# A decoder of thirteen stages on one core: choosing experts by halves of the tokens, beside the attention ahead and between blocks

## The chip, the cores and the metric

The kernel is one program on one core of a Trainium2 chip. The metric is device time in microseconds (us) from launch to end. TensorE (PE) multiplies, PEld is its weight load, DVE (VectorE), ACT (ScalarE) and POOL (GpSimd) work on rows, SP (SyncE) issues most transfers. POOL issues the indirect ones, with one address for each row.

## The reference

x has 16 sequences of 256 tokens of 128 numbers, so 4096 tokens, or 32 tiles of 128 tokens. Four layers follow each other, each of a self-attention, a cross-attention and a feed-forward part, with a residual and a layer norm after each part. Two of the feed-forward parts choose experts for each token:

```
# layer 1: 8 experts, 2 for each token; rows are first normalised
xh = (x - mean) / sqrt(var + 1e-6) * gamma[e] + beta[e]
out[e] = relu(xh @ W1[e] + b1[e]) @ W2[e] + b2[e] + x
y = sum over the 2 chosen e of softmax(top 2 of x @ Wg)[e] * out[e]
# layer 3: 16 experts, 4 for each token
logits = -|x - key|^2 + x @ rw.T + rb
y = sum over the 4 chosen e of softmax(top 4 of logits)[e] * (gelu(x @ w1[e] + b1[e]) @ w2[e] + b2[e])
```

## The kernel before, in words

`program` lists thirteen groups of stages. On every engine they run in that order, each stage waiting for `done` of the one before; each stage has one method for each engine, and an engine's instructions are executed in the order in which they are written. `s4` (CrossAttention) stands ahead of the two-of-eight experts `g5`, `s5`; `s11` (WideCross) ahead of the four-of-sixteen experts `g12`, `s12`. Both attentions are written as slots: slot g holds the scores of one piece, the softmax of an earlier one and the output product of a still earlier one. `s4` runs to slot 77, two slots for a batch; `s11` runs slots 6 to 36, one for a tile of 128 tokens. A `Tail` ends each attention: for a chunk c of four tiles the output product, the residual and moments on DVE (`dve_residual`), the inverse root on POOL by `newton` (`pool_root`), the norm on DVE (`dve_norm`), and the transposition into XT (`pe_turn`, `act_turn`). In `s4` chunk c has these in the slots 43 + 4c and after it; in `s11` the residual of chunk c is in slot 4c + 6.

`Gates` (L2212) does the choice for all 32 tiles at once: logits on TensorE as rows (L2262), transposed back (L2266), then on DVE softmax and `dve_choose`, which takes the largest logit, marks its first place and removes it, two or four times. `Dispatch.dve` (L2583 to L2632) makes slots of it: counts by TensorE, running sums over tiles, a first block for each expert (blocks of 128 rows, sorted by expert), and by `pick` the index of each chosen row. Two halves of 16 tiles are sorted separately but are computed together. `XHat` normalises the rows for the eight experts. After `Dispatch.dve` the b2 terms are put on X (L2296, L2303, L2484).

`ChosenExperts` then works in DRAM: `pool` (L3012) scatters rows of XT to L_sorted_rows, one indirect transfer for each tile and choice: 32 or 64 for each half. The first half's go out at once, the second half's one for each block (it waits for `xc`). Each half has NB = 39 or 79 blocks. SP loads a block (L3005); TensorE transposes it (L3049), multiplies it by W1 (L3057) and by W2 (L3066); DVE copies the block's expert out of the table of all experts (L3130) and the transposed rows (L3134, L3137); ACT applies the function (L3082) and copies the result (L3090), which SP stores. At last POOL gathers the results of each token (L3034) and DVE adds them (L3106), for the first half between blocks of the second.

## Time and profile before

| | us |
|---|---|
| median of 3 timed runs | 4725.97 (4720.38 to 4726.91) |
| the profiled execution | 4700.51 |
| its span | 4698.7 |
| TensorE busy | 3596.7 (77%) |
| DVE busy | 2838.3 (60%) |
| ACT busy | 2090.2 (44%) |
| POOL busy | 1134.3 (24%) |

The span runs from the first to the last instruction of one execution, on which the hardware profiler noted every instruction. Busy times can overlap between engines. What ended an idle time is inferred from semaphore events.

### The profile page before, as it was taken

How to read it: one execution, taken by the hardware profiler on the slowest of the kernel's cores; microseconds unless marked ns; L12 is line 12 of the kernel's file. 1: busy time of each engine (PE TensorE's matmuls, PEld its weight loads, DVE VectorE, ACT ScalarE, POOL GpSimd, SP SyncE). 2: the span in 40 equal slices, each digit the busy share in tenths (PEclk: the TensorE clock that was granted, in tenths of full speed). 3: DMA queues.
4: the chain of work that ended last, by engine and by line, in shares of the span. 5: the costliest groups of instructions: out<-in, count | busy, mean ns of one | idle time of the engine just before them, and what ended most of it. 6: DMA issues, size and time to landing. Idle time of an engine off the chain costs nothing. (4 is left out here: it accounts for less than half of the span.)

```text
span 4698.7 us, 87572 instructions
## 1 busy us (share of the span) xinstructions
PE 3596.7 (77%) x31326; PEld 2273.4 (48%) x31326; DVE 2838.3 (60%) x7553; ACT 2090.2 (44%) x4560; POOL 1134.3 (24%) x2203
## 2 busy tenths in 40 slices
PE   5877988877886758369898997579948979837980
PEld 2433553645553448224444453335526766617980
DVE  4974764547784645346776774477745568843453
ACT  2664655223434435136666664435611134414650
POOL 2322221021112254400111101243200041135346
PEclk9987998878986769669999997679968989958995
DMA  5323230112213142211112200423200030032232
GB/s 96 50 37 54 55 53 22 38 25 40 37 16 51 28 131 83 46 24 33 29 32 36 36 20 17 63 41 50 38 10 8 5 108 1 1 101 86 86 87 58
DMA packets 289737, 215.05 MB, mean 46 GB/s; under 512 B 43811, under 2 KB 274560, under 8 KB 289132
## 3 DMA queue, kind: packets, MB, share of 16 engines
q1 hardware_dynamic: 277020, 184.28, 20.4%
q0 software_dynamic: 12288, 25.19, 1.8%
q8 instruction: 253, 4.15, 0.4%
q14 instruction: 176, 1.44, 0.1%
HBM read 61.88 MB, written 45.69 MB: 23 GB/s over the span
## 5 line engine op out<-in xcount | busy, mean ns | idle before, releaser
L1316 ACT ACTIVATE PT<-ps 128x512 f32<-128x512 f32 (+1 forms) x1600 | 811.9, 559 | 513.1 <-PE ps L1376 270.9
L1266 DVE TENSOR_REDUCE M<-ps 128x2 f32<-128x512 f32 x1024 | 655.5, 684 | 288.5 <-PE ps L1250 260.8
L1229 PE MATMUL ps<-SKB 49*128 49x256 bf16 (+2 forms) x3584 | 433.9, 280 | 180.1 <-DMA SKB<-HH 81.2
L1263 DVE TENSOR_REDUCE M<-ps 128x3 f32<-128x384 f32 x768 | 390.6, 550 | 189.3 <-PE ps L1247 123.8
L1411 PE MATMUL ps<-PT,VA 128*9 128x256 f32 (+1 forms) x7168 | 449.9, 370 | 1.5 <-ACT PT L1316 1.0
L1356 PE MATMUL ps<-SKB 51*128 51x256 bf16 (+2 forms) x3584 | 366.2, 271 | 83.7 <-DMA SKB<-MT 65.5
L1229 PEld LDWEIGHTS ps<-SKB 48*128 48x128 bf16 (+1 forms) x3584 | 138.7, 95 | 484.2 <-issue 153.7
L3082 ACT ACTIVATE SKB<-ps,SKB 128x128 f32<-128x128 f32 x944 | 270.2, 371 | 201.6 <-PE ps L3057 186.6
L425 POOL TENSOR_TENSOR NW<-NW 128x4 f32<-128x4 f32 x336 | 70.8, 211 | 1014.9 <-DVE NW L418 987.8
L3130 DVE COPY SKB<-SKB 128x1028 f32 (+1 forms) x236 | 170.2, 721 | 225.6 <-PE ps L3066 127.5
L578 POOL TENSOR_TENSOR FF<-FF,HH 128x512 f32<-128x512 f32 (+1 forms) x118 | 128.8, 1092 | 605.2 <-ACT HH L567 605.0
L3066 PE MATMUL ps<-SKB 128*128 128x128 f32 x1888 | 256.0, 279 | 18.6 <-ACT SKB L3082 13.2
L3057 PE MATMUL ps<-SKB 128*128 128x128 f32 x1888 | 257.8, 281 | 0.0
L3023 POOL DMA_INDIRECT L_sorted_rows<-XT,RR x192 | 203.9, 1062 | 206.9 <-DVE RR L2623 81.6
L1411 PEld LDWEIGHTS ps<-PT,VA 128*9 128x9 f32 x7168 | 155.1, 91 | 199.8 <-issue 96.0
L3034 POOL DMA_INDIRECT SKB<-L_sorted_results,RR x192 | 192.4, 1002 | 235.4 <-DMA L_sorted_results<-SKB 101.7
L1356 PEld LDWEIGHTS ps<-SKB 50*128 50x128 bf16 (+1 forms) x3584 | 177.2, 98 | 143.3 <-DMA SKB<-MT 75.1
L3066 PEld LDWEIGHTS ps<-SKB 128*128 128x128 f32 x1888 | 234.1, 195 | 22.6 <-ACT SKB L3082 15.7
L3057 PEld LDWEIGHTS ps<-SKB 128*128 128x128 f32 x1888 | 235.7, 196 | 0.1
L2843 PEld LDWEIGHTS ps<-SKB 128*128 128x128 f32 x1536 | 187.8, 193 | 46.1 <-issue 45.9
L655 PE MATMUL ps<-idf,TV 128*128 128x128 f32 x1088 | 175.5, 285 | 34.4 <-ACT TV L646 17.4
L1307 ACT ACTIVATE PT<-ps 128x768 f32<-128x768 f32 x128 | 103.8, 811 | 210.0 <-DVE ps L1386 210.0
(369 smaller groups left out, 6995.6 us busy)
## 6 DMA issues: line engine op xcount, KB each, us to landing
SKB<-HH SPq DMA_DIRECT2D x1224, 64.0 KB
SKB<-HH SPq DMA_DIRECT2D x576, 32.0 KB
PT<-L_sorted_rows SPq DMA_DIRECT2D x236, 64.0 KB
L_sorted_results<-SKB SPq DMA_DIRECT2D x236, 64.0 KB
L_sorted_rows<-TV SPq DMA_DIRECT2D x2, 5056.0 KB, 30.9
SKB<-in_L3f_w SPq DMA_DIRECT2D x32, 256.0 KB
L_sorted_rows<-TV SPq DMA_DIRECT2D x2, 2496.0 KB, 15.5
SKB<-scratch SPq DMA_DIRECT2D x2, 2048.0 KB, 10.9
```

What stands on the lines that cost most here:

```text
L1229: k = e.matmul(self.mx_bank(m + i)[:, o:o + n], K.QS[self.set(c)][64 * i:64 * i + rows, s, 256 * bb + 128 * qt:256 * bb + 128 * qt + 128], ...
L1263: k = e.tensor_reduce(K.M3[n % 2][:, hh, 0:3], mx[:, 0:384].rearrange("p (a k) -> p a k", a=3), axis=AX.X, op=ALU.max)
L1266: k = e.tensor_reduce(K.M3[n % 2][:, hh, 0:2], mx.rearrange("p (a k) -> p a k", a=2), axis=AX.X, op=ALU.max)
L1316: e.activation(K.PT[:, x % 4, n * i:n * i + n], self.st_bank(x, i)[:, 0:n], ACT.Exp, bias=0.0, scale=self.scale).then_inc(*self.exp.inc())
L1356: k = e.matmul(self.st_bank(x, i)[:, 256 * kt:512 - lo if kt else 256], k1, q1, start=kt == 0, stop=plain and kt == 1)
L1411: k = e.matmul(K.PS[32 * i:32 * i + 9, 6, 256 * g + lo:256 * g + 256], K.VA[self.set(c)][:, (2 * bb + kt) * 16 + 8 * (i % 2) + 2 * j + i / ...
L2843: k = e.matmul(K.PS[:, 4 + m % 2, 128 * i:128 * i + 128], self.HB[m % 3][:, hc, 128 * i:128 * i + 128], self.WE[m // 8 % 3][:, 512 + 128 * ...
L3023: e.indirect_dma_start(self.XS[h], bass.IndirectOffsetOnAxis(ap=D.IDX[:, q:q + 1], axis=0), K.XT[:, 128 * t:128 * t + 128], None).then_inc ...
L3034: e.indirect_dma_start(self.YG[i % 8], None, self.YS[c // 4], bass.IndirectOffsetOnAxis(ap=D.IDX[:, q:q + 1], axis=0)).then_inc(*self.gath ...
L3057: k = e.matmul(K.PS[:, 2 + m % 2, 128 * hc:128 * hc + 128], self.WT[m % 3][:, 128 * hc:128 * hc + 128], self.XC[m % 3], start=True, stop=True)
L3066: k = e.matmul(K.PS[:, 4 + m % 2, 0:128], self.HB[m % 3][:, hc, :], self.WT[m % 3][:, 512 + 128 * hc:640 + 128 * hc], start=hc == 0, stop= ...
L3082: k = e.activation(self.HB[n % 3][:, hc, :], K.PS[:, 2 + n % 2, 128 * hc:128 * hc + 128], self.func, bias=self.WT[n % 3][:, 1024 + hc:1025 ...
```

## The change

The choice, the slots and the scatter are done for each half of the tokens by itself. `ChosenGates` takes the place of `Gates`, `Dispatch` and `XHat` for these two stages. Its work for each engine is a generator that is stepped. The steps of the first half stand in the last slots of the attention ahead (`at` is the first slot, `rate` the steps in a slot, `each` the scatters in a slot); those of the second half stand between blocks (`own` steps in a block). The logits come as 16 products with the tokens as weights, without transposition. The b2 terms, for the eight experts together with the scaling of X, stand between blocks 20 and 46. The second half's scatters no longer wait for blocks. The weights of the experts are loaded in slots of the attentions, and the zeros between sorted rows of the two-of-eight stage are written in the third group. Softmax, dispatch tables and gathered rows have other places in SBUF (`Room`). `WideCross.pool` is written by slots, so that scatters stand between the roots of the tail.

```diff
     def dve(self, e):
         self.join(e)
         for g in range(self.lead, self.slots):
+            if self.beside:
+                self.beside.dve_beside(e, g)
             self.dve_slot(e, g)
...
             self.pool_slot(e, g)
+            if self.beside:
+                self.beside.pool_beside(e, g)
...
+        if self.beside is not None:
+            if self.P + 16 <= g < self.P + 21:
+                self.beside.sp_expert(e, g - self.P - 16)
+            if g == self.P + 36:
+                e.wait_ge(*self.scored(6))
+                self.beside.sp_expert(e, 5)
+                self.beside.sp_expert(e, 6)
+            if g == self.P + 41:
+                e.wait_ge(*self.scored(7))
+                self.beside.sp_expert(e, 7)
...
+def choose(e, dv, G, v, best, removed, tiles, made=None):
+    E = G.E
+    sh = [128, tiles, E]
+    rev = G.rev[:, 0:E].rearrange("p (o e) -> p o e", o=1).to_broadcast(sh)
+    for k in range(G.top):
+        if k > 0:
+            e.tensor_reduce(G.ZE, v, axis=AX.X, op=ALU.max).then_inc(*dv.inc())
+            e.wait_ge(*dv.now())
+            best = G.ZE
+        e.tensor_tensor(G.EQ, v, spread(best, sh, "p (t o) -> p t o"), ALU.is_equal).then_inc(*dv.inc())
+        e.wait_ge(*dv.now())
+        e.tensor_tensor(G.FIRST, G.EQ, rev, ALU.mult).then_inc(*dv.inc())
+        e.wait_ge(*dv.now())
+        yield
+        e.tensor_reduce(G.Z, G.FIRST, axis=AX.X, op=ALU.max).then_inc(*dv.inc())
+        e.wait_ge(*dv.now())
+        e.tensor_tensor(G.OH[k], G.FIRST, spread(G.Z, sh, "p (t o) -> p t o"), ALU.is_equal).then_inc(*dv.inc())
+        e.wait_ge(*dv.now())
+        if k < G.top - 1:
+            left = G.LEFT[k % 2]
+            e.scalar_tensor_tensor(out=left, in0=G.OH[k], scalar=removed, in1=v, op0=ALU.mult, op1=ALU.add
+                                   ).then_inc(*dv.inc())
+            v = left
+        if k > 0:
+            o = e.tensor_tensor(G.MK, G.OH[0] if k == 1 else G.MK, G.OH[k], ALU.add)
+            if made and k == G.top - 1:
+                o.then_inc(*made.inc())
+            else:
+                o.then_inc(*dv.inc())
+        e.wait_ge(*dv.now())
+        yield
...
+        self.masked = 2 + 2 * top
+    def counts_at(self, gap):
+        return self.masked + max(gap, 7 if self.normed else 2)
+    def idx_at(self, gap, k):
+        return self.counts_at(gap) + 5 + k
...
+    def pe(self, e, h, gap):
+        K, W, E = self.K, self.W, self.E
+        n = 16 * E
+        e.wait_ge(*W.at)
+        if self.router:
+            e.wait_ge(*self.router.made.at(0))
+        gw = self.router.gw if self.router else W["gw"]
+        pj = K.pj_take(e)
+        if self.router and h == 0:
+            e.matmul(pj[:, n:n + E], W["one"], self.router.sq, start=True, stop=True)
+        for i in range(16):
+            t = 16 * h + i
+            if i % 4 == 0:
+                e.wait_ge(*self.ahead.tail.xt.at(t // 4))
+            k = e.matmul(pj[:, E * i:E * i + E], K.XT[:, 128 * t:128 * t + 128], gw, start=True, stop=True)
+        k.then_inc(*self.lmm.inc())
+        K.pj = self.lg.at(h)
+        for _ in range(self.counts_at(gap)):
+            yield
+        e.wait_ge(*self.mask.at(h))
+        pj = K.pj_take(e)
+        mk = self.MK.rearrange("p t e -> p (t e)")
+        e.matmul(pj[:, 0:n], W["triu"], mk, start=True, stop=True)
+        e.matmul(pj[:, 256:256 + n], W["one"], mk, start=True, stop=True).then_inc(*self.counted.inc())
+        K.pj = self.read.at(h)
...
+    def act(self, e, h, gap):
+        K = self.K
+        yield
+        e.wait_ge(*self.sub.at(h))
+        e.activation(self.EX, self.EX, ACT.Exp, bias=0.0, scale=1.0).then_inc(*self.exp.inc())
+        if self.normed:
+            for _ in range(self.counts_at(gap)):
+                yield
+            e.wait_ge(*self.root.at(h))
+        e.wait_ge(*self.lmm.at(h))
+        for c in range(4 * h, 4 * h + 4):
+            if self.normed:
+                for t in range(4 * c, 4 * c + 4):
+                    i = t - 16 * h
+                    k = e.activation(K.XT[:, 128 * t:128 * t + 128], K.X[:, t, :], ACT.Identity,
+                                     bias=self.SHIFT[:, i:i + 1], scale=self.RSD[:, i:i + 1])
+            else:
+                k = e.activation(K.xt(c).rearrange("p (a b) -> p a b", a=4), K.xc(c), ACT.Copy, bias=0.0, scale=1.0)
+            if c % 4 == 3:
+                k.then_inc(*self.rows.inc())
+            yield
...
+    def dve(self, e, h, gap):
+        K, W, E, dv = self.K, self.W, self.E, self.K.dv
+        sh = [128, 16, E]
+        e.wait_ge(*self.lmm.at(h))
+        logits = K.PS[:, 7, 0:16 * E].rearrange("p (t e) -> p t e", t=16)
+        if self.router:
+            if h == 0:
+                e.tensor_tensor(W["rbb"], W["rbb"], K.PS[:, 7, 16 * E:17 * E], ALU.add).then_inc(*dv.inc())
+                e.wait_ge(*dv.now())
+            e.tensor_tensor(self.LG, logits, W["rbb"].rearrange("p (o e) -> p o e", o=1).to_broadcast(sh), ALU.add
+                            ).then_inc(*self.lg.inc())
+        else:
+            e.tensor_copy(self.LG, logits).then_inc(*self.lg.inc())
+        e.wait_ge(*self.lg.at(h))
+        yield
+        e.tensor_reduce(self.S1, self.LG, axis=AX.X, op=ALU.max).then_inc(*dv.inc())
+        e.wait_ge(*dv.now())
+        e.tensor_tensor(self.EX, self.LG, spread(self.S1, sh, "p (t o) -> p t o"), ALU.subtract).then_inc(*self.sub.inc())
+        yield
+        for _ in choose(e, dv, self, self.LG, self.S1, NEG, 16, self.mask):
+            yield
+        e.wait_ge(*self.mask.at(h))
+        e.wait_ge(*self.exp.at(h))
+        e.tensor_tensor(self.EX, self.EX, self.MK, ALU.mult).then_inc(*dv.inc())
+        e.wait_ge(*dv.now())
+        e.tensor_reduce(self.S1, self.EX, axis=AX.X, op=ALU.add).then_inc(*dv.inc())
+        e.wait_ge(*dv.now())
+        yield
+        e.reciprocal(self.S2, self.S1).then_inc(*dv.inc())
+        e.wait_ge(*dv.now())
+        e.tensor_tensor(self.gates(h), self.EX, spread(self.S2, sh, "p (t o) -> p t o"), ALU.mult).then_inc(*self.g.inc())
...
+            e.wait_ge(*self.ahead.tail.x.at(4 * h + 3))
+            for part in range(4):
+                for i in range(8 * (part % 2), 8 * (part % 2) + 8):
+                    if part < 2:
+                        k = e.bn_stats(self.ST[:, i, :], K.X[:, 16 * h + i, :])
+                    else:
+                        k = e.bn_aggr(self.MV[:, i, :], self.ST[:, i, :])
+                k.then_inc(*dv.inc())
+                e.wait_ge(*dv.now())
+                yield
+            if h == 1:
+                e.wait_ge(*self.root.at(0))
+            root_seed(e, K, self.NW[:, 0, :], self.NW[:, 1, :], self.MV[:, :, 1], 1e-6).then_inc(*self.seed.inc())
...
+            pk = self.PK[:, 16 * k:16 * k + 16]
+            self.pick(e, k, by_expert(pos), pk)
+            e.tensor_copy(self.IDX[:, col], pk).then_inc(*self.idx.inc())
+            yield
...
+    def pe_beside(self, e, g):
+        if g >= self.at:
+            self.step("pe", self.D.pe(e, 0, 2 * self.rate), self.rate)
+    def act_beside(self, e, g):
+        if g > self.at:
+            self.step("act", self.D.act(e, 0, 2 * self.rate), self.rate)
+    def dve_beside(self, e, g):
+        if g == self.at - 1:
+            self.D.dve_first(e)
+        if g > self.at:
+            self.step("dve", self.D.dve(e, 0, 2 * self.rate), self.rate)
+    def pool_beside(self, e, g):
+        if g > self.at:
+            self.step("pool", self.pool_first(e), 1)
+    def pool_first(self, e):
+        D, top, gap = self.D, self.top, 2 * self.rate
+        seeded, n = (D.counts_at(gap) - 1) // self.rate, 0
+        while n < D.idx_at(gap, 0) // self.rate:
+            if n == seeded and D.normed:
+                D.pool_root(e, 0)
+            yield
+            n += 1
+        for i in range(16 * top):
+            if i > 0 and i % self.each == 0:
+                yield
+            self.pool_scatter(e, 0, i)
+    def pool_scatter(self, e, h, i):
+        K, D = self.K, self.D
+        k, t = i // 16, 16 * h + i % 16
+        if i == 0:
+            e.wait_ge(*self.zeroed.at(0))
+            e.wait_ge(*D.rows.at(h))
+        if i % 16 == 0:
+            e.wait_ge(*D.idx.at(self.top * h + k))
+        q = 32 * k + t
+        e.indirect_dma_start(self.XS[h], bass.IndirectOffsetOnAxis(ap=D.IDX[:, q:q + 1], axis=0),
+                             K.XT[:, 128 * t:128 * t + 128], None).then_inc(self.scattered[h].sem, 16)
...
+        self.rest("pool")
+        if D.normed:
+            D.pool_root(e, 1)
+        for i in range(16 * top):
+            self.pool_scatter(e, 1, i)
...
+            if n >= 1:
+                for _ in range(self.own):
+                    next(second, None)
+            c = self.b2_at.get(n)
+            if c is not None:
+                self.pe_gates_turn(e, c)
+            c = self.b2_at.get(n - 3)
+            if c is not None:
+                self.pe_b2(e, c)
...
+    def dve_b2(self, e, c):
+        K, D = self.K, self.D
+        pj = K.PS[:, 7, :].rearrange("p (a b) -> p a b", a=4)
+        e.wait_ge(*self.b2.at(c))
+        e.wait_ge(*D.rows.at(c // 4))
+        if self.normed:
+            for i in range(4):
+                t = 4 * c + i
+                k = e.scalar_tensor_tensor(out=K.X[:, t, :], in0=K.X[:, t, :], scalar=D.SG[:, t:t + 1], in1=pj[:, i, :],
+                                           op0=ALU.mult, op1=ALU.add)
+        else:
+            k = e.tensor_tensor(K.xc(c), K.xc(c), pj, ALU.add)
+        k.then_inc(*self.x.inc())
...
+            if n == NB:
+                for _ in second:
+                    pass
+            if n % NB == 0:
+                e.wait_ge(*self.D.blocks.at(n // NB))
...
+            if 2 <= n < NB:
+                for _ in range(self.own):
+                    next(second, None)
+            c = self.b2_at.get(n - 5)
+            if c is not None:
+                self.dve_b2(e, c)
...
+        o = self.o
+        e.wait_ge(*self.abc.at(3))
+        e.wait_ge(*self.tail.biased.at(7))
+        for x in (0, 1, 2):
+            self.beside.sp_expert(e, x)
+        e.wait_ge(*o.at(23))
+        for x in (12, 13):
+            self.beside.sp_expert(e, x)
+        e.wait_ge(*self.u.at(31))
+        e.wait_ge(*self.st.at(27))
+        for x in (3, 4, 14, 15):
+            self.beside.sp_expert(e, x)
+        e.wait_ge(*o.at(27))
+        self.beside.sp_expert(e, 8)
+        e.wait_ge(*self.st.at(31))
+        for x in (5, 6, 7):
+            self.beside.sp_expert(e, x)
+        e.wait_ge(*o.at(31))
+        for x in (9, 10, 11):
+            self.beside.sp_expert(e, x)
...
-        for c in range(8):
-            self.tail.pool_root(e, c)
+        for g in range(6, 37):
+            if g % 4 == 2:
+                self.tail.pool_root(e, g // 4 - 1)
+            if self.beside:
+                self.beside.pool_beside(e, g)
...
-        g5 = Gates(K, s4, W[5], 8, "L1", top=2)
-        s5 = ChosenExperts(K, g5, W[5], g5.dispatch, ("L1f_w1", "L1f_w2", "L1f_b1"), ACT.Relu)
+        g5 = ChosenGates(K, s4, W[5], 8, "L1", 2, Room([K.SKB[:, 10240:14336]]), None)
+        s5 = ChosenExperts(K, s4, W[5], g5, ("L1f_w1", "L1f_w2", "L1f_b1"), ACT.Relu, at=59, rate=3, each=3, own=2)
...
-        g12 = Gates(K, s11, W[12], 16, "L3", top=4)
-        s12 = ChosenExperts(K, g12, W[12], g12.dispatch, ("L3f_w1", "L3f_w2", "L3f_b1"), ACT.Gelu, last=True)
-        groups = ((s0,), (s1,), (g2, s2), (s3,), (s4,), (g5, s5), (s6,), (s7,), (s8,), (g9, c9, s9), (s10,), (s11,),
-                  (g12, s12))[:stop]
+        room = Room([K.GG[:, :]] + [t[:, :] for t in K.OT] + [v[:, :, :].rearrange("p a b -> p (a b)") for v in K.VA]
+                    + [K.BIG[:, 8192:10520]])
+        g12 = ChosenGates(K, s11, W[12], 16, "L3", 4, room, K.HH[0][:, :, :].rearrange("p a b -> p (a b)"))
+        s12 = ChosenExperts(K, s11, W[12], g12, ("L3f_w1", "L3f_w2", "L3f_b1"), ACT.Gelu, at=21, rate=4, each=5, own=1,
+                            last=True)
...
+        s4.beside = s5 if stop > 5 else None
+        s11.beside = s12 if stop > 12 else None
...
-                if n == 5:
-                    s4.done(e)
+                if n == 2 and stop > 5:
+                    s1.done(e)
                     s5.pool_zero(e)
...
-                if n == 12:
-                    W[n].load(e)
-                if n == 5:
-                    s5.sp_zero(e)
+                if n == 11 and stop > 12:
+                    W[12].load(e)
...
+                if n == 2 and stop > 5:
+                    s5.sp_zero(e)
```

## Rows read from the trace of the kernel before

**Rows 1.** The page, part 1: busy us, share of the span, instructions.
```profile
PE 3596.7 (77%) x31326; PEld 2273.4 (48%) x31326; DVE 2838.3 (60%) x7553; ACT 2090.2 (44%) x4560; POOL 1134.3 (24%) x2203
```

**Rows 2.** Busy time by stretch: us, each engine, PE clock, DMA share, GB/s.
```profile
1598.70:1640.50 41.80, 22.69 (x170) 13.13 (x169) 20.84 (x92) 13.80 (x29) 9.55 (x48) 0.76 0.01 1
1640.50:1676.70 36.20, 21.63 (x84) 9.93 (x84) 23.82 (x117) 19.18 (x44) 3.88 (x15) 0.64 0.90 275
1676.70:1727.30 50.60, 16.30 (x66) 12.06 (x65) 18.96 (x54) 2.94 (x5) 37.19 (x32) 0.50 0.14 47
1727.30:1811.00 83.70, 83.30 (x720) 82.78 (x721) 48.09 (x87) 55.06 (x209) 39.27 (x34) 0.97 0.31 94
...
4112.00:4168.40 56.40, 21.54 (x86) 8.78 (x86) 31.99 (x68) 12.19 (x17) 0.00 (x0) 0.62 0.49 158
4168.40:4255.00 86.60, 15.94 (x65) 12.20 (x65) 21.14 (x30) 2.35 (x4) 64.09 (x64) 0.50 0.15 50
4255.00:4424.00 169.00, 163.59 (x1422) 162.58 (x1422) 80.33 (x168) 110.26 (x415) 69.19 (x68) 0.97 0.31 93
```

**Rows 3.** Order of time, start and us: scatters and blocks begin.
```profile
1676.70 1.22 POOL L3023 DMA_INDIRECT L_sorted_rows<-XT,RR  x1 [22.09 <-DVE RR L2623]
...
1727.32 0.66 PE L3049 MATMUL ps<-idf,PT 128*128 128x128 f32 x2 [20.42 <-issue]
...
4168.44 1.07 POOL L3023 DMA_INDIRECT L_sorted_rows<-XT,RR  x1 [59.54 <-DVE RR L2623]
...
4250.76 0.96 POOL L3023 DMA_INDIRECT L_sorted_rows<-XT,RR  x1 [0.31 <-issue]
...
4254.99 1.36 PE L3049 MATMUL ps<-idf,PT 128*128 128x128 f32 x3 [51.92 <-DMA PT<-L_sorted_rows]
```

**Rows 4.** Order of time: DVE in the last slots of both attentions.
```profile
1616.31 1.11 DVE L337 TENSOR_SCALAR X<-RR,MV,RSD 128x128 f32<-128x128 f32 x4 [2.48 <-POOL RSD L431]
...
4074.68 1.22 DVE L3530 TENSOR_REDUCE M<-PT 128x16 f32<-128x1024 f32 x1 [1.12 <-ACT PT L3523]
...
4088.94 0.17 DVE L418 TENSOR_SCALAR NW<-NW 128x4 int32<-128x4 int32 x1
...
4105.36 0.17 DVE L418 TENSOR_SCALAR NW<-NW 128x4 int32<-128x4 int32 x1
...
4108.93 1.12 DVE L337 TENSOR_SCALAR X<-RR,MV,RSD 128x128 f32<-128x128 f32 x4 [3.40 <-POOL RSD L431]
```

**Rows 5.** Order of time: operations of the choice on DVE.
```profile
1640.51 6.29 DVE L2743 BATCH_NORM_STATS2 SKB<-X 128x6 f32<-128x128 f32 x32 [1.95 <-issue]
...
1654.83 0.42 DVE L2374 TENSOR_TENSOR PT<-PT,SKB 128x256 f32<-128x256 f32 x1
...
1671.44 0.28 DVE L2590 TENSOR_TENSOR SKB<-SKB 128x128 f32<-128x128 f32 x1
...
4180.90 1.46 DVE L2628 TENSOR_TENSOR SKB<-RR,WB 1x1264 f32<-1x1264 f32 x1
```

**Rows 6.** Order of time: the expert copy on DVE among blocks.
```profile
1728.54 0.70 DVE L3130 COPY SKB<-SKB 128x1030 f32 x1 [0.32 <-issue]
...
1756.69 0.70 DVE L3130 COPY SKB<-SKB 128x1030 f32 x1 [0.68 <-issue]
...
4330.59 0.85 DVE L3130 COPY SKB<-SKB 128x1028 f32 x1 [0.89 <-issue]
...
4332.48 0.88 DVE L3130 COPY SKB<-SKB 128x1028 f32 x1 [0.85 <-issue]
```

**Rows 7.** A scatter and a table load (start, us); waits (total, times, longest).
```profile
1683.40 7.04 POOL L3023 DMA_INDIRECT L_sorted_rows<-XT,RR  x1 [0.30 <-issue]
...
4262.00 1.28 ACT L3082 ACT_TABLE_LOAD   x1 [61.06 <-remote]
...
DVE X L2484 <- remote: 48.3, 5, 14.7
DVE SKB L3130 <- remote: 31.5, 12, 3.5
```

491 lines of the change are left out of this document (246 added, 245 removed).

## The prediction

> **What bounds the kernel now.** I read the page first, then the table of stretches around the two stages with chosen experts, then the order of time in them, then the waits. The page [rows 1] says only that TensorE is busiest and no engine is full: shares over thirteen stages decide nothing. The stretches do [rows 2]. Between the attention and the two-of-eight experts nothing overlaps: 36.2 us in which DVE chooses (23.8 busy), then 50.6 us in which POOL scatters (37.2 busy) and TensorE waits. Before the four-of-sixteen experts the same two parts take 56.4 and 86.6 us. The attentions end at 1640.5 and 4112.0; POOL's first scatters start at 1676.70 and 4168.44, TensorE's first blocks at 1727.32 and 4254.99 [rows 3], which ends the two stretches. So two heads of 86.8 and 143.0 us, 229.8 in all, are what can be hidden. The blocks behind are TensorE's: 83.3 of 83.7 us busy, and 163.6 of 169.0 [rows 2], a block each 1.89 us (4332.48 - 4330.59) [rows 6]. Whatever is put between blocks costs once the little slack there is used. The gathers that end the kernel are not touched.
>
> **The change part by part.** *One half's choice on DVE.* Half of the tokens makes operations of 256 elements with sixteen experts and of 128 with eight: 0.42 and 0.28 us, 0.04 between them [rows 5]. Sixteen experts, four chosen: 25 operations of the choice, 5 of the weights, 10 of copying, running sums and positions, 16 of the picks, 56 x 0.46 = 26; some 22 small ones at 0.2 make 4; the block table 2 x 1.46 = 3: 33 us, 23 of them before the first index. Eight experts, two chosen: 34 x 0.32 = 11, small ones 3.5, table 1, and 16 of the 32 statistics, 16/32 of 6.29 and about 1 = 4: 19.5 us. The whole choice is thus not less DVE work than before, only cut in two.
>
> *First half in the wide attention (slots 22 to 30 of 36).* DVE is the bound there: 1.12 us of idle in about every second slot of 6.3 us [rows 4]. Of the 23 us before the first index some 3 vanish in it. The step stands at the head of slot 27, which began at 4074.68 - 12.6 = 4062: first scatter at 4082 instead of 4168. A scatter takes (4250.76 - 4168.44)/63 = 1.31 us [rows 3]; beside DVE's long operations I take 1.5. POOL, in its written order, issues 15 (4104), then waits for the seed of chunk 6, which DVE's inserted work moves from 4088.94 by 28 to 4117; the root is 3.4 us (4105.53 to 4108.93) [rows 4]; 20 scatters to 4147; the root of chunk 7, whose seed (4105.36, then 4133) has been waiting, to 4151; the last 29 to 4189. From last scatter to first block it was 4.2 us [rows 3]: 4193. The attention itself ends at 4155, covered by the scatters. Gain 62 us.
>
> *First half in the attention ahead (slots 60 to 67).* DVE is busy 20.8 of the last 41.8 us [rows 2], so much of the 19.5 fits, but not in slots 60 to 62, and DVE's order puts steps ahead of the norm: 3 us for the first slots, 4 for the norm of chunk 5, 2 for ACT waiting for the root of the row norms. The norm of chunk 5 stood at 1616.31 [rows 4], slot 66 a microsecond later: first scatter at 1627. Six scatters 1635, root of chunk 6 1638.5, twelve 1654, root of chunk 7 1657.5, fourteen 1676, first block 1680. Gain 47 us.
>
> *Second half between blocks.* DVE waits 0.85 us in a block of the last stage and 0.68 in the other, of which 0.32 stays even when nothing holds it [rows 6]: slack 0.53 and 0.36 us. Last stage: 33 blocks with a step each, 33 - 33 x 0.53 = 15 us. Other: 12 blocks with two, 19.5 - 12 x 0.36 = 15. TensorE gets 16 products for the logits, two counts and, for b2, 8 x 12 records; a block is 17 records in 1.89, so 0.11 each: 10.7 for b2, 5 for the rest, per stage. In the last stage half of it lies beside DVE-bound blocks (8 with DVE's b2 sum); in the other, where b2 falls into TensorE-bound blocks, 13. Exp between Gelus on ACT: two table loads of 1.28 us [rows 7]: 3. Together 26 and 28, 54 us. Bounds: with perfect packing 36; with no overlap at all 33 + 19.5 + 31 + 3 + 14 for DVE's b2 sums (8 of 512 elements, 0.7 us by the same line, and 32 of 128) = 100.
>
> *Trains of scatters beside critical work.* The second scatters are no longer one per block but back to back, 32 and 64, 126 us at 1.31. No row shows such a train beside blocks. From below it costs nothing: 38 scatters, one per block, left TensorE 97% busy [rows 2]. From above, rows 7: with trains running, DVE's b2 sum waited 48.3 us in five waits that no engine ended, of 137 us of scattering (50.6 + 86.6), and one scatter took 7.04 us beside unbroken DVE work. Nearest are the gathers in bursts of eight among blocks: the expert copy waited 31.5 us in twelve such waits. I take 15 us, both ends kept.
>
> The Trainium skill, "SBUF — State Buffer", section on the two physically separate sides with its box on DVE blocking SWDGE, says that DVE and GpSimd share one port pair by exclusive lock, and that a two-port copy keeps GpSimd from writing descriptors. The 7.04 us scatter [rows 7] agrees; the one at 4168.44, which ran beside DVE's picks in 1.07 us [rows 3], does not show it. By that rule each expert copy and train exclude each other, which is the second rival below.
>
> *Moved and free.* Expert weights (24 x 0.53 MB), issued by SP, go into attention slots whose DMA share is 0.01, so they leave the heads; SP's waits for freed parts of the tile stand behind the last stacks, so nothing is late. If they queued ahead of a shift's transfer, 0.53 MB at the 158 GB/s of the head, 3 us, and the scores need it two slots later. Zero stores go to the third stage, behind its strips and beside its last experts. Gates, the logits' transposes and 32 row scalings in the heads vanish: they lay under the scatter and pay nothing. The second half is scattered before block 39 or 79 is due (it ends about block 34 and 62). TensorE's granted clock was 0.76 where it was busy 22.7 of 41.8 us and 0.97 in the blocks [rows 2]. Blocks that wait for DVE leave it 1.9 of some 3.0 us, so part of them will be at 1.2 GHz; their records then take about DVE's pace, which I leave unpriced and cover by the range.
>
> **The sum.** 62 + 47 = 109 gained, 54 + 15 = 69 paid: 40 us. The profiled execution took 4700.51 (span 4698.7), so 4660.5; the median of the timed runs is 4725.97, 25 us above it, and I keep that distance: 4686 us. Own range: paid 50 to 85, gain 24 to 59, 4667 to 4702.
>
> **The rivals.** *Packing is better.* Paid 36 and nothing for the trains: gain 73, 4653. For it: steps are cut small, and two blocks of buffering even them out. Against: TensorE is 97% busy already.
>
> *The trains wait with DVE (slower).* If during the 126 us of second scatters DVE gets through only each 10 to 15 us, as the sum's longest wait of 14.7 says, blocks stand for the train's whole length: gain 109 - 54 - 126 = -71, 4797. It decides slower once the trains stop the blocks for more than 55 of 126 us. For it: rows 7. Against: DVE picked on beside the first scatters of the head [rows 3], and the expert copies among gathers waited 3.5 us at the most. In its milder form, waits of 48.3/137 of the train's length, it takes 44 us instead of 15: gain 11, 4715.
>
> *The head is not hidden.* If POOL in slots 27 to 36 gets hardly a scatter in because DVE's 1.22 us operations follow one another, 50 scatters start at 4125 only: 4125 + 64 x 1.31 + 7 + 4 = 4220, 27 us later; with 5 us in the other stage the gain is 8, 4718.
>
> **How the numbers follow.** Forecast 0.55, better packing 0.17, mild trains 0.12, head not hidden 0.06, trains that stop the blocks 0.10. A measurement tells 0.2%, 9.5 us, from no change. Faster (under 4716.5): 0.55 + 0.17 + 0.07 + 0.02 = 0.81; same 0.09; slower 0.10. Eight in ten: 4640 (better packing and 13 us more) to 4728, leaving out the stopped blocks and a tail below.
>
> **What would show it.** First scatters about 1627 and 4082 (the latter 14 earlier by what the first stage gains, 47 - 28 - 5); no stretch of over 10 us without TensorE between attention and blocks but some 22 us in the first and 38 in the last stage; first blocks at 1680, and 4193 - 14 = 4179. Expert copies 2.4 us apart in the last stage's first 35 blocks and 3.0 in the other's first 13, later 1.9. Unexplained waits of DVE under 25 us in the trains. Wrong would be: scatters of several microseconds in the attention, blocks stretched to 5 us and more, or an attention that ends after its scatters do.

## The result, and the profile after

The changed kernel is slower: 4803.81 us (4797.35 to 4805.70, 4 runs) against 4726.44 us (4720.38 to 4728.93, 4 runs), ratio 1.0163 [1.0146, 1.0181], where 4686 was forecast. The profiled execution took 4803.26 us around a span of 4801.4, so it stands at its median; that of before stood 25 us under its own. Between the two spans lie 102.7 us, between the medians 77.4, so up to 25 us of what the traces show below come from that quick execution of before. Later runs on chips 5, 8, 11 and 15 (the number of the first run's chip is not known) split this result: on chip 8 it came again, 1.0164, and on chip 15 the same kernel is *faster*, 0.9961 and 0.9952.

The page of the kernel after, part 1, answers to [rows 1]: TensorE's busy time rose by 29 us, its share fell.

```profile
PE 3625.6 (76%) x31366; PEld 2314.0 (48%) x31366; DVE 2841.9 (59%) x7683; ACT 2080.0 (43%) x4552; POOL 1118.5 (23%) x2217
```

The view of busy time by stretch, kernel after (columns as in [rows 2]). Lines one to four are the two-of-eight stage: the tail of the attention, the wait for scatters, blocks beside the second half's choice, the second half's scatters. The last four are the same of the four-of-sixteen stage.

```profile
1640.50:1677.40 36.90, 11.22 (x54) 6.97 (x52) 10.81 (x46) 9.00 (x22) 23.37 (x43) 0.55 0.14 47
1677.40:1697.40 20.00, 1.26 (x5) 0.90 (x5) 0.95 (x3) 0.60 (x1) 12.74 (x13) 0.50 0.29 86
1697.40:1744.10 46.70, 36.70 (x238) 35.16 (x238) 29.49 (x112) 21.24 (x75) 3.77 (x14) 0.80 0.13 37
1744.10:1789.80 45.70, 16.28 (x100) 14.75 (x99) 7.03 (x16) 7.24 (x28) 31.81 (x32) 0.64 0.18 60
...
4155.40:4198.40 43.00, 16.91 (x108) 14.68 (x106) 20.25 (x46) 7.14 (x8) 26.45 (x45) 0.70 0.38 117
4198.40:4238.60 40.20, 2.21 (x9) 1.59 (x9) 1.02 (x3) 0.60 (x1) 27.26 (x29) 0.50 0.16 55
4238.60:4296.40 57.80, 49.38 (x368) 46.97 (x368) 35.08 (x99) 31.11 (x104) 0.00 (x0) 0.91 0.16 45
4296.40:4383.10 86.70, 16.48 (x85) 12.99 (x84) 8.16 (x18) 5.39 (x21) 61.75 (x64) 0.56 0.16 54
```

In the fourth line of each stage POOL issues a train, that is scatters one right after the other, and TensorE, which should do blocks, is busy for 16 us of 46 and of 87. The heads are mostly hidden, as meant: the order of time in the kernel after, first scatter and first block of both stages, against [rows 3].

```profile
1646.96 1.21 POOL L3149 DMA_INDIRECT L_sorted_rows<-XT,SKB  x1 [8.86 <-ACT XT L2880]
...
1697.23 0.91 PE L3218 MATMUL ps<-idf,PT 128*128 128x128 f32 x2 [18.61 <-DMA PT<-L_sorted_rows]
...
4130.73 1.07 POOL L3149 DMA_INDIRECT L_sorted_rows<-XT,SKB  x1 [1.14 <-DVE SKB L3017]
...
4237.48 0.91 PE L3218 MATMUL ps<-idf,PT 128*128 128x128 f32 x2 [37.81 <-DMA PT<-L_sorted_rows]
```

Since everything before a stage moves its absolute times (the two executions are 6.3 us apart at the first mark; on chip 15 it is 1.4), I compare distances. Each is in us from SP's issue of a weight load in the same stage or just ahead of it (the gate weights of the two-of-eight stage; the linear attention's `wkv`), in the profiled execution named. Chip 15 ran both kernels side by side.

| from the mark | before | after | before, chip 15 | after, chip 15 |
|---|---|---|---|---|
| two of eight: attention ends | 123.0 | 155.5 | 119.6 | 155.7 |
| first block | 211.8 | 175.4 | 207.4 | 175.6 |
| block 40 (second half) | 284.7 | 318.5 | 280.8 | 283.2 |
| last block | 384.5 | 422.0 | 369.4 | 376.3 |
| four of sixteen: attention ends | 664.0 | 711.1 | 666.7 | 711.3 |
| first block | 809.0 | 750.2 | 811.5 | 750.5 |
| block 80 (second half) | 964.3 | 1016.8 | 960.4 | 938.4 |
| last block | 1141.6 | 1203.4 | 1121.2 | 1100.9 |

First blocks come 36.4 and 58.8 us earlier, 95.2 gained. Blocks 1 to 40 then take 143.1 instead of 72.9 us and blocks 1 to 80 take 266.6 instead of 155.3; second halves take 3.7 and 9.3 more: 194.5 paid. Net 99.3 of the 102.7 between the spans.

Where it is lost, in the order of time (kernel after, DVE's expert copy, one a block):

```profile
1716.88 0.70 DVE L3366 COPY SKB<-SKB 128x1030 f32 x1 [0.44 <-issue]
1720.00 0.70 DVE L3366 COPY SKB<-SKB 128x1030 f32 x1 [0.76 <-DVE SKB L2936]
...
1768.75 0.70 DVE L3366 COPY SKB<-SKB 128x1030 f32 x1 [12.26 <-issue]
1789.85 0.70 DVE L3366 COPY SKB<-SKB 128x1030 f32 x1 [19.89 <-remote]
...
4301.58 0.73 DVE L3366 COPY SKB<-SKB 128x1028 f32 x1 [0.33 <-issue]
4313.69 0.70 DVE L3366 COPY SKB<-SKB 128x1028 f32 x1 [10.19 <-remote]
4383.10 0.70 DVE L3366 COPY SKB<-SKB 128x1028 f32 x1 [67.14 <-remote]
```

The first pair is choice between blocks: 3.12 us a block instead of 1.9 [rows 6]. The others are stops: two blocks in 81.5 us. "Remote" means that the profile found no releaser. TensorE's and ScalarE's rows in the same stretch lead to it. Here x1 or x8 is the number of matmuls in the row:

```profile
4317.84 0.37 PE L3226 MATMUL ps<-SKB 128*128 128x128 f32 x1 [1.78 <-issue]
4319.24 0.37 PE L3226 MATMUL ps<-SKB 128*128 128x128 f32 x1 [1.03 <-issue]
...
4323.44 0.37 PE L3226 MATMUL ps<-SKB 128*128 128x128 f32 x1 [1.03 <-issue]
4325.54 0.37 PE L3226 MATMUL ps<-SKB 128*128 128x128 f32 x1 [1.73 <-issue]
4363.20 2.08 PE L3235 MATMUL ps<-SKB 128*128 128x128 f32 x8 [37.29 <-issue]
```
```profile
4362.01 1.14 ACT L3306 ACTIVATE SKB<-ps,SKB 128x128 f32<-128x128 f32 x4 [48.14 <-remote]
4383.01 0.28 ACT L3314 ACTIVATE SKB<-ps 128x128 f32<-128x128 f32 x1 [19.86 <-remote]
```

Matmuls of one block that otherwise start 0.11 us apart start 1.40 us apart and more, waiting for nothing the profile shows; scatters start 1.26 us apart. ScalarE can use their result only at 4362.0, 36 us after the last of them (4325.54 + 0.37) by the profile, whose ends of matmuls are modelled. The scatters end at 4377.4. So in this stretch TensorE stops; ScalarE waits for it, and DVE, SP and in the end TensorE wait in a ring. Transfers are not what is late: the packets of SP's store and load issued at 4313.90 and 4314.26 had moved by 4316. The scatters keep their 0.96 us throughout and the long stop has no copy in it: it isn't DVE and GpSimd that shut each other out. The Trainium skill's rule on that ("SBUF — State Buffer", the section on the two physically separate sides), cited in the prediction, is not what these rows show. The scatter of 7.04 us [rows 7], which the prediction laid to that rule, came on chip 15 too, again in 7.04 us beside the same 8.49 us of DVE work, where no train stops anything: it is another effect, and prices no train. Whether DVE, given work, would have been slowed as TensorE was, these rows can't tell; a later experiment does.

### The profile page after: what moved, and what is told of

Its sections match the earlier page's. It is cut to its first block and busy times, and to the rows that moved or that the text cites. A ratio compares the mean times of both kernels' runs of the same rounds, so it can differ in the third digit from the quotient of the medians.

```text
span 4801.4 us, 87829 instructions
## 1 busy us (share of the span) xinstructions
PE 3625.6 (76%) x31366; PEld 2314.0 (48%) x31366; DVE 2841.9 (59%) x7683; ACT 2080.0 (43%) x4552; POOL 1118.5 (23%) x2217
## 5 line engine op out<-in xcount | busy, mean ns | idle before, releaser
L3235 PE MATMUL ps<-SKB 128*128 128x128 f32 x1888 | 267.7, 287 | 82.9 <-issue 44.9
L3235 PEld LDWEIGHTS ps<-SKB 128*128 128x128 f32 x1888 | 244.2, 202 | 88.7 <-issue 46.3
L3201 POOL DMA_INDIRECT PT<-L_sorted_results,SKB x192 | 191.7, 999 | 394.0 <-DMA L_sorted_results<-SKB 249.9
L3226 PE MATMUL ps<-SKB 128*128 128x128 f32 x1888 | 271.3, 289 | 9.3 <-issue 9.3
L3226 PEld LDWEIGHTS ps<-SKB 128*128 128x128 f32 x1888 | 247.5, 204 | 10.1 <-issue 9.9
L3149 POOL DMA_INDIRECT L_sorted_rows<-XT,SKB x192 | 188.3, 981 | 137.6 <-DVE SKB L3017 63.4
L2663 PEld LDWEIGHTS ps<-SKB 128*128 128x128 f32 x1536 | 186.3, 192 | 46.1 <-issue 45.8
## 6 DMA issues: line engine op xcount, KB each, us to landing
L_sorted_rows<-TV SPq DMA_DIRECT2D x2, 2496.0 KB, 20.4
```

Source lines behind the costliest of these rows:

```text
L2663: k = e.matmul(K.PS[:, 4 + m % 2, 128 * i:128 * i + 128], self.HB[m % 3][:, hc, 128 * i:128 * i + 128], self.WE[m // 8 % 3][:, 512 + 128 * ...
L3149: e.indirect_dma_start(self.XS[h], bass.IndirectOffsetOnAxis(ap=D.IDX[:, q:q + 1], axis=0), K.XT[:, 128 * t:128 * t + 128], None).then_inc ...
L3201: e.indirect_dma_start(self.YG[i % 8], None, self.YS[c // 4], bass.IndirectOffsetOnAxis(ap=D.IDX[:, q:q + 1], axis=0)).then_inc(*self.gath ...
L3226: k = e.matmul(K.PS[:, 2 + m % 2, 128 * hc:128 * hc + 128], self.WT[m % 3][:, 128 * hc:128 * hc + 128], self.XC[m % 3], start=True, stop=True)
L3235: k = e.matmul(K.PS[:, 4 + m % 2, 0:128], self.HB[m % 3][:, hc, :], self.WT[m % 3][:, 512 + 128 * hc:640 + 128 * hc], start=hc == 0, stop= ...
```

## The experiments

Theory A: scatters issued back to back stop TensorE. Rivals: B, each scatter costs blocks the same wherever it lies; C, pacing (letting each scatter go only when a given block is done) only moves the wait. A burst is a short train. Ratios are to the kernel before on the same chip, with 95% intervals.

**Pace the second half's scatters** (chip 5).
```
         for i in range(16 * top):
+            e.wait_ge(*self.xc.at(self.ready + i * (self.NB - 2 - self.ready) // (16 * top)))   # ready: 12 and 21
             self.pool_scatter(e, 1, i)
```


> The changed kernel, but the second half's scatters are paced: scatter i waits until block ready + i*(NB-2-ready)/count has been turned and copied (one per 1.9 us block or fewer), in both stages. Theory A (scatters issued back to back stop TensorE, so that DVE and ScalarE wait 'remote'; one alone between blocks costs nothing): the stops of 20 us (two-of-eight) and 67+10 us (four-of-sixteen) in the DVE's waits for the expert copy go, 'remote' there falls from 134.5 us to under 30, and the time falls by 85 to 115 us to 4690 to 4720. Rival B (every scatter costs the blocks about 1.1 us of TensorE or DMA wherever it lies): the same 96 scatters cost the same 100 us in small pieces, the time stays 4780 to 4810. Rival C (pacing only makes the second half start late): the blocks run at 1.9 us but a gap of 20 to 60 us stands before the second half's first block; 4730 to 4770.

0.9970 [0.9958, 0.9981]; no remote wait at the expert copy. In this ratio it lies where A put it, and alone it would have looked like proof of A; in microseconds, 4658, it lies below every forecast.

**Bursts of 8** (chip 5): `i` in the wait above becomes `i - i % 8`.

> As the paced kernel, but the same scatters come in bursts of 8 back to back, each burst let go by the block at which its first would have come (4 bursts and 8 bursts). Theory A: each burst of 8 stops TensorE for about 5 to 7 us (the before kernel's bursts of four indirect DMAs show TensorE's signals 1.4 to 2.4 us late), so 12 bursts cost 50 to 90 us against the paced kernel, in pieces of 5 to 8 us. Rival B: the same time as paced and as the changed kernel.

0.9965 [0.9951, 0.9979], again no stop. A had promised 50 to 90 us.

**A pause between unpaced scatters** (chip 5): one memset after each scatter, in the second half alone.
```
             self.pool_scatter(e, 1, i)
+            e.memset(K.TV[:, 0:512], 0.0).then_inc(*K.po.inc())
+            e.wait_ge(*K.po.now())
```


> The changed kernel, unpaced second half, but GpSimd writes a 128x512 tile (one memset, no DMA) between two scatters, so that they come some 1.8 to 2.4 us apart without any tie to the blocks. Theory A (it is back-to-back issue that stops TensorE): the stops of 20 and 77 us go or shrink to a third though the train is unpaced, and the time is 4690 to 4740. If what counts is that GpSimd is never idle, whatever it does, or that the scatters are not tied to the blocks, the stops stay and grow with the train (+60 us): 4820 to 4880.

0.9975 [0.9965, 0.9984].

**Plain DMAs** (chip 5). This version leaves out the sorting of the second half.
```
+        if h == 1:
+            e.dma_start(self.XS[h][128 * i:128 * i + 128, :], K.XT[:, 128 * t:128 * t + 128]
+                        ).then_inc(self.scattered[h].sem, 16)
+            return
...
```


> The changed kernel, but the second half's scatters are plain DMAs from GpSimd's queue: 128 rows to 128 rows in order, not to the chosen slots (so the rows of the second half are not sorted; everything else as before). It tells whether the indirect form matters. Theory A1 (descriptors that GpSimd makes in software for any DMA, back to back): the same stops, 4790 to 4810. Theory A2 (only the indirect form, which reads an index for each row, stops TensorE): no stops, 4690 to 4725.

0.9975 [0.9965, 0.9985]. Four different edits, one result, and the kernel before at 4669 us instead of 4726: chip 5 could not tell the theories apart, and the change itself has not run there. So theory D: the stops belong to the chip.

**The change itself, and the kernel before, for a trace** (chip 15).

> The changed kernel itself, unaltered, as a control beside the others of this call, since the kernel before was 1.2% quicker in the first four experiments' call than beside the first run of the change. If the stops of 20 and 77 us in the trains belong to the kernel (theory A), they are here again and the ratio is 1.014 to 1.020. If they belong to the chip on which it ran (theory D: there one kernel's unpaced train is stopped, here it isn't), 'remote' at the expert copy is under 30 us and the ratio is 0.995 to 1.000, as for the four variants.

> The kernel before, unaltered, for its trace on this call's chip: the ratio is 1.000 by construction. It is to show which stages are shorter where the kernel before takes 4669 us than where it takes 4726: by theory D the head before its first block (in the first trace 86.8 and 143.0 us, with 48.3 us of 'remote' waits of DVE beside the scatters) and the block stages, by a theory of a quicker clock all TensorE-bound stages alike.

0.9961 [0.9947, 0.9976] and 1.0005 [0.9994, 1.0017]. Theory D holds: the same kernel that lost 77 us gains 17. The kernel before is quicker here in the stages with indirect DMAs and hardly elsewhere: its last blocks come 15.1 and 20.4 us earlier from the marks (table). What A missed is that the stops need both the train and the kind of chip. (Chip 15 ran at two times with one result, chips 5, 8 and 11 once each; that it is the chip and not the moment is read from this, not shown.) Busy time by stretch in the change on chip 15, both trains of scatters beside blocks:

```profile
1740.00:1783.80 43.80, 42.04 (x361) 40.10 (x361) 24.80 (x53) 26.52 (x100) 34.07 (x32) 1.00 0.34 103
...
4251.70:4336.80 85.10, 81.63 (x673) 77.82 (x672) 46.38 (x98) 48.26 (x179) 65.59 (x64) 0.96 0.33 102
```

TensorE is busy for 42.0 of 43.8 and 81.6 of 85.1 us beside trains of the same length (34.1 and 65.6 us of POOL) that leave it 16 us elsewhere.

**Gathers paced too** (chip 15; scatters in bursts of 8).
```
+                if c < 4:
+                    e.wait_ge(*self.xc.at(self.NB + 8 + i * (self.NB - 14) // (16 * top)))
                 e.indirect_dma_start(self.YG[i % 8], None, ...
```


> The kernel with the second half's scatters in bursts of 8, and the first half's gathers paced too, one let go per block in place of bursts of four. In the traces each burst of four gathers goes with a block of 3.3 to 5.2 us. If back-to-back issue is what stretches them, the second half's blocks run at 1.9 to 2.1 us each: 10 to 25 us less than the same kernel with gathers in bursts (ratio to before 0.992 to 0.995). If it is the sum's own work on DVE between the blocks, nothing: 0.996 to 0.997.

0.9959 [0.9946, 0.9971]: nothing gained against the change. The second half of the last stage took 161.2 us against 162.5.

**First half's scatters held until the attention has issued its work** (chip 15; scatters of the second half in bursts of 8): in `pool_first`, 64 times `yield` ahead of the scatters.

> The kernel with bursts of 8, but the first half's scatters are kept until the attention ahead has issued all its own work; choice and slots stay between its slots. If scatters in the attention's tail are what lengthens it (its end moved from 1640.5 to 1677 and, less the shift, from 4112 to 4155), the attentions end 15 to 35 us earlier and the 32 and 64 scatters (1.26 us each, 40 and 81 us) follow them: first blocks 5 to 10 and 15 to 30 us later than with scatters inside, ratio 1.001 to 1.006. If it is DVE's choice that lengthens them, the ends stay and the scatters' 20 and 40 us inside the attention are lost: ratio 1.005 to 1.012.

1.0056 [1.0039, 1.0073]. From the marks the attentions end at 145.7 and 697.6. So of their lengthening on chip 15 (36.1 and 44.6 us), the scatters make 10.0 and 13.7, less than the 15 to 35 expected, and what stays with them held, the choice above all, 26.1 and 30.9. First blocks come 13.5 and 30.5 us later: letting scatters into the attention is worth it. This kernel's last norm of the attention, first scatter and first block in the last stage:

```profile
4148.94 1.12 DVE L337 TENSOR_SCALAR X<-RR,MV,RSD 128x128 f32<-128x128 f32 x4 [3.40 <-POOL RSD L431]
...
4149.44 1.07 POOL L3150 DMA_INDIRECT L_sorted_rows<-XT,SKB  x1 [0.54 <-issue]
...
4233.42 0.86 PE L3221 MATMUL ps<-idf,PT 128*128 128x128 f32 x2 [82.12 <-DMA PT<-L_sorted_rows]
```

**The second half's choice in the wait for the first half's scatters** (chip 15).
```
 pe, dve:  second = self.D.pe(e, 1, ...)            # dve the same
+          for _ in second:
+              pass                                  # ahead of the blocks, not one step a block
 act:     +for _ in range(self.D.counts_at(2 * self.own) + 1 if self.normed else 8):
+              next(second, None)
 pool:    +e.wait_ge(*self.xc.at(1 + 7 * i // 8))    # ahead of scatter i of the second half
```


> The changed kernel with the second half's choice and slots moved once more: out of the blocks into the stretch between the attention's end and the first block, where DVE stands idle for the first half's scatters (17.8 us in the two-of-eight stage, 37.5 us in the four-of-sixteen), and the second half's scatters one per block from block 1 on. If choice between blocks is what the blocks pay (39 scatter-free blocks took 34.3 us longer and 79 took 39.1 us longer than in the kernel before on the same chip), 50 to 70 us go and the ratio to before falls from 0.996 to 0.981 to 0.987. If the blocks pay for the scatters beside them instead, at most 15 us go: 0.993 to 0.996. If the second half's choice pushes the first block back by its own length, nothing goes: 0.995 to 1.000.

0.9912 [0.9889, 0.9935]: a smaller gain than the 0.981 to 0.987 hoped for and a larger one than the rival's 0.993, so neither account has the size. It is under the change, which ran beside it (medians 22.5 us apart, and the times of the two don't overlap):

> The changed kernel again, a control. If this call's chip is of the kind on which the kernel before takes some 4725 us, theory A (trains of scatters stop TensorE there) says ratio 1.014 to 1.020 with 'remote' waits of DVE over 100 us at the expert copy; where the kernel before takes some 4670 us, ratio 0.995 to 0.998 and under 30 us, as in the call before. Any other pairing of the two (a slow before with a quick change) breaks the theory that the same property of the chip makes both.

> The change with the second half's scatters one per block, again. On a chip where the trains stop TensorE, theory A says that pacing alone brings the ratio from 1.016 down to 0.995 to 1.002. On the other kind of chip it is worth nothing (0.996 to 0.998), as on the first chip that had it.

0.9952 [0.9933, 0.9971] and 0.9969 [0.9955, 0.9983], the change and the paced change. In the last stage block 80 comes 913.7 us from the mark instead of 937.5 (the change beside it) and blocks among the first 35 are 2.13 us apart instead of 2.75; the two-of-eight stage's block 40 comes at 271.1 instead of 282.6. The wait for scatters had held room for the whole second choice. Its first blocks on TensorE:

```profile
4177.89 1.03 PE L3221 MATMUL ps<-idf,PT 128*128 128x128 f32 x2 [15.95 <-DMA PT<-L_sorted_rows]
4180.90 0.45 PE L3221 MATMUL ps<-idf,PT 128*128 128x128 f32 x1 [1.99 <-DVE SKB L3380]
```

The wait for the first block's rows is 16.0 us where it was 37.9 (4193.10 in the change on chip 15).

**On chip 8, before at 4716 us.** Three kernels side by side: the change as control, the bursts of 8, and the last version (second choice in the wait, scatters one per block) with gathers paced as well.

> The changed kernel, as the control of this call. Before near 4725 us: ratio 1.014 to 1.020, DVE's 'remote' waits at the expert copy above 100 us. Before near 4670 us: ratio 0.994 to 0.998, none.

> The second half's scatters in bursts of 8. Where trains stop TensorE (before near 4725 us), each of the 12 bursts costs 5 to 7 us by theory A (the first few of a train are free, then TensorE stands until its end): ratio 1.002 to 1.010, between paced and unpaced. If what counts is only the total of scatters beside blocks, 1.014 to 1.018. Where the kernel before takes 4670 us: 0.995 to 0.998, as before.

> The kernel with the second half's choice in the wait for the first half's scatters, and besides the first half's gathers paced one by one over the second half's blocks. Where the kernel before takes 4670 us, pacing gathers was worth nothing in sum (0.9959 against 0.9965), so this should be 0.988 to 0.993 as without it. Where the kernel before takes some 4725 us, its bursts of four gathers held TensorE's signals back by 1.4 to 2.4 us each, so that there the pacing gives 10 to 30 us more: 0.978 to 0.990. The rival (paced gathers finish later than bursts and push the end) gives 0.994 to 0.998 on either.

1.0164 [1.0132, 1.0196], 1.0082 [1.0063, 1.0102] and 0.9886 [0.9864, 0.9907]. The first result is reproduced, and here the form of the train sets the price. What DVE waited for ahead of the expert copy (us, times), in the change, in the bursts of 8:

```profile
  PE ps L3235: 159.3, 133
  remote: 146.2, 21
```
```profile
  PE ps L3238: 165.4, 113
  remote: 101.5, 34
```

Blocks 1 to 80 took 259.6, 233.9 and (last version) 177.9 us; on chip 15 the change took 187.9. Over that, a burst costs (233.9 - 187.9)/8 = 5.8 us, as expected, and the one train of 64 costs 71.7. Against the same burst version on chip 5 (186.9) it is 5.9 a burst. The first burst is nearly free, the later ones are not. The sixth in the order of time, scatters and then expert copies:

```profile
4395.03 0.96 POOL L3150 DMA_INDIRECT L_sorted_rows<-XT,SKB  x1 [11.43 <-DVE SKB L3376]
...
4404.33 0.95 POOL L3150 DMA_INDIRECT L_sorted_rows<-XT,SKB  x1 [0.30 <-issue]
4415.60 0.95 POOL L3150 DMA_INDIRECT L_sorted_rows<-XT,SKB  x1 [10.31 <-DVE SKB L3376]
```
```profile
4395.75 0.73 DVE L3369 COPY SKB<-SKB 128x1028 f32 x1 [1.00 <-PE ps L3238]
4398.66 0.70 DVE L3369 COPY SKB<-SKB 128x1028 f32 x1 [1.99 <-PE ps L3238]
4402.34 0.86 DVE L3369 COPY SKB<-SKB 128x1028 f32 x1 [2.78 <-remote]
4406.71 0.70 DVE L3369 COPY SKB<-SKB 128x1028 f32 x1 [3.31 <-remote]
4409.00 0.70 DVE L3369 COPY SKB<-SKB 128x1028 f32 x1 [1.40 <-PE ps L3238]
```

Four blocks take 13.3 us, where the same four on chip 5 take 7.6. Bursts against one train would leave a weaker B alive, one in which each scatter costs something wherever it lies. The last version closes it: the same 64 indirect scatters, one per block on the same chip, cost the blocks 4.1 us (165.8 from the third expert copy to the 80th, 161.7 on chip 15), and DVE's remote waits at the copy in these blocks are 2.1 us in it and 75.9 in the change. C is out as well: no gap stands before the second half's first block, whose expert copy comes 1.9 us after the one before.

The last version also shows that it isn't TensorE alone. Its second choice runs on DVE beside the last unbroken scatters of the first half. Small copies of the running sum, on chip 15 and then on chip 8:

```profile
4166.11 0.15 DVE L2999 COPY VA<-VA 128x1 f32<-128x1 f32 x1
4166.38 0.29 DVE L2999 COPY SKB<-VA 128x2 f32<-128x2 f32 x1
```
```profile
4202.03 0.15 DVE L2999 COPY VA<-VA 128x1 f32<-128x1 f32 x1 [1.18 <-issue]
4203.43 0.17 DVE L2999 COPY SKB<-VA 128x2 f32<-128x2 f32 x1 [1.17 <-DVE VA L3000]
```

They start 0.27 us apart on chip 15 and 1.40 us apart on chip 8; 1.40 us is also the pace at which TensorE's matmuls started above. The chain from L2993 to L3005 takes 1.4 us on chip 15 and 7.7 on chip 8, though its operations last as long, and the third expert copy comes 14.4 us after the first block's transposition instead of 3.6. So theory A is too narrow: beside a train, DVE is slowed too.

**On chip 11, before at 4712 us.** Pause, plain form, and the last version without paced gathers.

> The changed kernel, second half unpaced, one GpSimd memset of 128x512 between two scatters. Where the kernel before takes over 4710 us: if TensorE is stopped by indirect DMAs issued without a pause, the stops of 20 and 80 us go and the ratio is 0.998 to 1.006; if a busy GpSimd is enough, they stay or grow with the train: 1.016 to 1.030. Where the kernel before takes 4670 us: 0.996 to 0.999, as the first time, and nothing is told apart.

> The changed kernel with the second half's scatters as plain DMAs of GpSimd (rows in order, so the second half isn't sorted). Where the kernel before takes over 4710 us: if the descriptors of any GpSimd DMA stop TensorE, 1.010 to 1.018; if it takes the indirect form, 0.998 to 1.004. Where it takes 4670 us: 0.996 to 0.999.

> The second half's choice in the wait for the first half's scatters, its scatters one per block, gathers in bursts of four. Where the kernel before takes over 4710 us: 5 to 20 us more than the version with paced gathers, so 0.990 to 0.994. Where it takes 4670 us: 0.989 to 0.993, as the first time.

0.9954 [0.9937, 0.9971], 0.9957 [0.9939, 0.9975], 0.9927 [0.9907, 0.9947]. The first two gain more than was expected of a chip of chip 8's kind. The change itself did not run on chip 11; that it is of that kind is read from the kernel before's time and from gathers in bursts of four, in the second halves, beside which all of DVE's remote waits lie (ahead of the expert copy, version with the pause; chips 5 and 15 have none):

```profile
  PE ps L3237: 141.4, 106
  remote: 30.8, 12
```

In the version with the pause the same 64 indirect scatters ran untied to blocks on a GpSimd that never rests. The order of time there, POOL and TensorE:

```profile
4258.25 0.96 POOL L3149 DMA_INDIRECT L_sorted_rows<-XT,SKB  x1 [0.28 <-POOL TV L3192]
4259.21 0.54 POOL L3192 MEMSET TV<- 128x512 f32 x1
4260.03 1.10 POOL L3149 DMA_INDIRECT L_sorted_rows<-XT,SKB  x1 [0.28 <-POOL TV L3192]
```
```profile
4265.34 1.06 PE L3237 MATMUL ps<-SKB 128*128 128x128 f32 x8
4266.23 0.27 PE L3220 MATMUL ps<-idf,PT 128*128 128x128 f32 x1
4266.34 1.06 PE L3228 MATMUL ps<-SKB 128*128 128x128 f32 x8
```

Scatters 1.8 us apart (2.0 on average) and matmuls in rows of eight in 1.06 us: blocks 1 to 80 took 189.7 us, and 191.4 in the same version on chip 5. If chip 11 is of chip 8's kind, a pause of 0.8 us is enough, and neither a busy GpSimd nor the tie to the blocks matters. Plain DMAs, 0.6 us apart (64 in 38.3 us), don't stop TensorE either (187.6 us, 187.7 on chip 5), though that train was half as long, so form and length are not parted. And pacing the gathers, worth nothing on chip 15, is worth 16.6 us in the last stage on chip 8: its second half took 165.5 us with it and 182.1 in the change beside it (179.2 without it on chip 11).

## Why the prediction was wrong

- *Heads, right in the last stage.* 62 and 47 us forecast, 58.8 and 36.4 measured (61.0 and 31.8 on chip 15). In the two-of-eight stage the first scatter was due at 1627 and came at 1646.96, 6.3 us of it the execution's shift. ScalarE's sixteen scalings of rows had to follow the root (1637.7) and stood between the attention's own work, so that they ended at 1646.1, where I had 2 us; DVE's and POOL's inserted work made the attention 32.5 us longer where I had 19.5 us of DVE fitting into its gaps. Of the signs of being wrong, "an attention that ends after its scatters do" did not come; "blocks stretched to 5 us and more" did, up to 69 us.
- *Second half between blocks, sized too low.* 28 and 26 us forecast; chip 15, where no train stops anything, gives 38.7 and 40.7 (blocks of both halves). Blocks were 3.2 and 2.75 us apart against 3.0 and 2.4. On chip 15 TensorE's 32 logit records took 6.9 us, 0.22 each, where 0.11 was taken from full blocks: they come behind the wait for scatters, in which TensorE stands, at a granted clock of 0.50 (stretch 1677.40 to 1697.40 above; 0.50 too in chip 15's 1693.6 to 1702.0), the lower of its two levels, 1.2 GHz. The rest I lay to DVE's choice and b2 sums, which fitted less well than the slack promised; no run parts them.
- *Trains of scatters beside blocks: the step that failed.* I took 15 us, "both ends kept". It measured 194.5 - 79.4 = 115.1 us between the first chip's pair of traces and chip 15's (35.2 and 79.9); by the medians, which are free of the quick execution of before, the two pairs differ by 77.4 + 16.6 = 94.0 us, and chip 8's and chip 15's by 88.3. The row that priced it was there: DVE's b2 sum waited 48.3 us in five waits that no engine ended, beside the same trains [rows 7]. In the kernel before on chip 15 the b2 sum has no such wait; TensorE ended all of its waits (us, times, longest):

```profile
DVE X L2484 <- PE ps L2303: 41.9, 20, 4.0
```

So those five were TensorE's results coming late. I spread them over the scattering and then took a lighter row as nearest, of gathers "in bursts of eight"; but only the first eight come together, the others in fours. And [rows 7] came from a stage in which little else ran; in blocks each such stop holds four engines. The "38 scatters, one per block" that left TensorE 97% busy (there are 64 in that stage) were paced, and pace, as the bursts, the pause and the last version show, makes the difference.
- *The rival.* "The trains wait with DVE" forecast 4797 at a chance of 0.10; 4803.8 came. Its place was right and its size near, its mechanism not: DVE does not shut out GpSimd, TensorE stops. That the time came so close is in part luck: its terms were 109, 54 and 126, those of the traces 95, 79 and 115, and the sum of these, -99, is not the -77 of the medians either.
- *The range.* 4640 to 4728 left that rival out because one reading of a price was preferred, though its price of 126 us would alone have turned the sign. On the other kind of chip the forecast's sign is right and its size still over: 0.9961 against 4686/4726 = 0.9915.

The version that beats both kernels is the second choice in the wait, scatters one per block and gathers paced: 0.9886 on the chip where the change is 1.0164. With the gathers paced it ran on chip 8 alone; without, it is 0.9912 on chip 15 and 0.9927 on chip 11.

## What to carry to other kernels

Taking a pacing wait out of a queue of indirect DMAs is an edit of its own: price the train beside the work that it will run beside, from the "remote" waits of the trace, however idle the stage that shows them. Look for work to move into a wait before moving it between saturated blocks: the wait for the first scatters was as long as the whole second choice. And time a change on more than one chip; the kernel before, run beside it, took 4716 us on chip 8, which shows the stops, and 4670 to 4673 on chip 15, which doesn't.

## What the runs showed of the hardware

- On some chips (the first run's, chip 8 and, by the signs above, chip 11) indirect DMAs that GpSimd issues 1.26 us apart slow the engines beside them: TensorE starts a matmul only every 1.40 us and its results are used up to 36 us late, and a chain of small DVE operations takes 7.7 us instead of 1.4. On chip 15 a train of 64 costs the blocks nothing (187.9 us, 190.0 with scatters paced), and chip 5 showed no stop in bursts of eight. One scatter per block costs 4.1 us for 64 on chip 8; scatters with a pause between, 2.0 us apart on average, cost nothing on chips 5 and 11.
- Durations do not differ between the kinds: a scatter has a median of 0.96 us and a copy one of 0.70 in the traces of the change on both. Nor does the granted clock in stages that the change leaves alone (0.89 and 0.90 from 2100 to 3300 us); in the stop it is 0.56, where chip 15 has 0.96. What in the chip makes the difference stays open; the traces show late starts and late results, not why.
- In the trace of before the same thing was there at small size. The kernel before takes 4716 and 4712 us on chips 8 and 11 against 4669 and 4673 on 5 and 15, 0.8 to 1.0% more. Where that lies is shown for the first run's chip alone: of 36.0 us between its trace and chip 15's, 35.5 are in the two stages with indirect DMAs, 27.7 of them in second halves, where gathers go in fours.
